# Who makes the low part of the last tile's x3: two halves on VectorE in place of GpSimd

## What is computed

```
x = x + L0(x)   # gate/up/silu/down, each with rank-16 adapters picked per batch
x = x + L1(x)   # W = weights[condition]; einsum('bct,bcd->bdt', x, W): 32 x 32 per batch
x = x + L2(x)   # x @ W.T plus SCALING * (top-2 of 8 experts, rank 16, softmax gates)
x = x + L3(x)   # as L1, with its own 16 matrices of 32 x 32
```

## Time and profile before

| | us |
|---|---|
| median of 3 runs | 585.18 |
| lowest and highest of them | 585.09, 585.28 |
| the profiled execution, as timed | 585.28 |
| its span in the profile | 583.0 |
| TensorE busy | 568.0 (97% of the span) |
| VectorE busy | 302.7 (52%) |
| ScalarE busy | 205.4 (35%) |
| GpSimd busy | 225.0 (39%) |

### The profile page before, as it was taken

How to read it: one execution, slowest core, us unless ns; L and a number is a source line. 1 busy time by engine, 2 the same in 40 slices (tenths; PEclk the granted TensorE clock), 3 DMA queues, 4 the chain that set the end, 5 groups by cost and what they waited for, 6 DMA issues and landing times.

```text
span 583.0 us, 8797 instructions
## 1 busy us (share of the span) xinstructions
PE 568.0 (97%) x3371; PEld 512.3 (88%) x3371; DVE 302.7 (52%) x695; ACT 205.4 (35%) x413; POOL 225.0 (39%) x229
## 2 busy tenths in 40 slices
PE   5989999999999999999999999999999999999996
PEld 4778998988889898989898989898989899999994
DVE  4896353535353534344444444444444657778775
ACT  4764242323233333333232323323232533333321
POOL 5442143556565656441313131413130212433422
PEclk9999999999999999999999999999999999999998
DMA  8992333343434343442424242424242911243322
GB/s 269 374 320 70 109 123 115 101 154 125 151 131 154 126 153 121 151 152 78 137 76 138 76 137 76 136 77 136 76 137 73 329 53 54 83 154 109 126 74 73
DMA packets 34889, 77.38 MB, mean 133 GB/s; under 512 B 5216, under 2 KB 9632, under 8 KB 34848
## 3 DMA queue, kind: packets, MB, share of 16 engines
q0 software_dynamic: 10752, 37.23, 20.4%
q1 hardware_dynamic: 23952, 39.56, 20.1%
q10 hardware_dynamic: 144, 0.03, 0.0%
HBM read 64.22 MB, written 12.58 MB: 132 GB/s over the span
## 4 chain that ended last, share of the span: by engine, by line
PE 94%; DMA 2%; DVE 2%; ACT 1%; issue 0%; POOL 0%; SPq 0%; DVEq 0%
PE gu_ps L1139 14%; PE gu_ps L1141 14%; PE gu_ps L1140 13%; PE down_ps L1139 8%; PE down_ps L1140 8%; PE down_ps L1141 8%; PE l_ps L1139 5%; PE l_ps L1140 5%; PE l_ps L1141 5%; PE gu_ps L1146 3%; PE gu_ps L1147 3%; PE act_t L1209 3%; DMA b_sel_raw<-b_gu,idx_rank 1%; PE x2t_ps L1263 1%; PE down_ps L1147 1%; PE down_ps L1146 1%
## 5 line engine op out<-in xcount | busy, mean ns | idle before, releaser
L666 POOL DMA_INDIRECT b_sel_raw<-b_gu,idx_rank x48 | 47.6, 992 | 189.5 <-PE gu_ps L1147 176.6
L1139 PE MATMUL gu_ps<-w_sb,xt 128*128 128x512 f32 x256 | 104.7, 409 | 0.7 <-DVE w_sb L932 0.7
L1139 PE MATMUL down_ps<-wd_sb,act_hl 128*128 128x288 f32 (+1 forms) x352 | 105.1, 299 | 0.0
L1140 PE MATMUL down_ps<-wd_sb,act_hl 128*128 128x288 f32 (+1 forms) x352 | 103.7, 295 | 0.0
L1141 PE MATMUL down_ps<-wd_sb,act_hl 128*128 128x288 f32 (+1 forms) x352 | 103.6, 294 | 0.0
L1141 PE MATMUL gu_ps<-w_sb,xt 128*128 128x512 f32 x256 | 100.6, 393 | 0.0
L1140 PE MATMUL gu_ps<-w_sb,xt 128*128 128x512 f32 x256 | 100.2, 391 | 0.0
L666 POOL DMA_INDIRECT a_raw<-a_all,idx_batch x64 | 76.5, 1195 | 58.0 <-DVE wd_sb L932 38.1
L784 ACT CAST act_hl<-act_t 128x256 fp32r<-128x256 f32 (+1 forms) x64 | 27.3, 452 | 134.6 <-PE act_t L1209 130.6
L775 ACT ACTIVATE act<-gu_ps 128x512 f32<-128x512 f32 (+1 forms) x47 | 26.1, 555 | 126.5 <-PE gu_ps L1147 126.5
L932 DVE TENSOR_TENSOR act_hl<-act_t,act_hl 128x256 fp32r<-128x256 f32 (+1 forms) x64 | 32.0, 520 | 71.8 <-ACT act_hl L784 71.0
(11 more groups left out here) (146 smaller groups left out, 1107.3 us busy)
## 6 DMA issues: line engine op xcount, KB each, us to landing
w_sb_raw<-wgu SPq DMA_DIRECT2D x16, 256.0 KB, 10.6
x_res<-x_rows SPq DMA_DIRECT2D x16, 256.0 KB
x_after_l<-x_res SPq DMA_DIRECT2D x16, 256.0 KB
bd<-bd_hl SPq DMA_DIRECT2D x16, 256.0 KB
x<-x_after_l SPq DMA_DIRECT2D x16, 256.0 KB, 2.7
bd_hl<-bd SPq DMA_DIRECT2D x16, 256.0 KB, 4.0
xt_raw<-x_t SPq DMA_DIRECT2D x15, 256.0 KB
out<-y SPq DMA_DIRECT2D x15, 256.0 KB, 2.0
```

Source lines behind the costliest of these rows:

```text
L666: nc.gpsimd.indirect_dma_start(out=dst, out_offset=None, in_=table, in_offset=bass.IndirectOffsetOnAxis(ap=idx, axis=0)).then_inc(s, 16)
L1139: pe.matmul(out_, stationary[0], moving[0], start=start, stop=False, skip_group_check=True)
L1140: pe.matmul(out_, stationary[0], moving[1], start=False, stop=False, skip_group_check=True)
```

## The change

GpSimd's `low_x3` no longer knows pieces, and its call for the last tile is gone. A new function of VectorE, `low_last_x3`, makes both halves for tile 15. It waits for the high half (s_x3hi) and, for the first half, for GpSimd's low part of tile 14 (s_x3lo at 15); for the second half it waits for its own first half (s_x3lo at 16), so that s_x3lo counts in order as before. It stands between add_x3(15) and add_y(14) in VectorE's queue.

```diff
             def low_x3(t):
-                for n, (a, b) in enumerate(pieces(t)):
-                    pool.wait_ge(s_x3hi, t + n + 1)
-                    pool.tensor_tensor(x3_hl[:, t % 2, 1, a:b], x3[:, t % 3, a:b],
-                                       x3_hl[:, t % 2, 0, a:b].bitcast(F32), ALU.subtract).then_inc(s_x3lo, 1)
+                pool.wait_ge(s_x3hi, t + 1)
+                pool.tensor_tensor(x3_hl[:, t % 2, 1, :], x3[:, t % 3, :],
+                                   x3_hl[:, t % 2, 0, :].bitcast(F32), ALU.subtract).then_inc(s_x3lo, 1)
...
                 if t < NT:
                     low_x1(t)
-            low_x3(NT - 1)
...
+            def low_last_x3():
+
+                t = NT - 1
+                for n, (a, b) in enumerate(pieces(t)):
+                    ve.wait_ge(s_x3hi, t + n + 1)
+                    ve.wait_ge(s_x3lo, t + n)
+                    ve.tensor_tensor(x3_hl[:, t % 2, 1, a:b], x3[:, t % 3, a:b],
+                                     x3_hl[:, t % 2, 0, a:b].bitcast(F32), ALU.subtract).then_inc(s_x3lo, 1)
+
...
             add_y(NT - 3)
             add_x3(NT - 1)
+            low_last_x3()
             add_y(NT - 2)
             add_y(NT - 1)
```

## The result

| | before | changed |
|---|---|---|
| median, us | 585.23 (585.09 to 585.33, 6 runs) | 583.12 (582.38 to 584.41, 6 runs) |
| ratio to before | | 0.9971, 95% interval 0.9961 to 0.9981 |
| the profiled execution, us | 585.28 | 584.41 |
| its span, us | 583.0 | 582.5 |

The changed kernel is faster by 1.7 us by the ratio (0.0029 x 585.2, interval 1.1 to 2.3) and by 2.1 us by the medians. The prediction said no change, 584.85 to 585.5.

The account below looks back on a forecast made before the run. TensorE carries 94% of the chain, but the end hangs on y of tile 14's store: 0.16 us less TensorE wait, 0.00 arriving, plus 0.84 us VectorE work hidden in idle time, gives 585.2 us, no change; range 584.85 to 585.5.

Parts of the forecast that it names:

- The end hangs on the moment at which y of tile 14 is stored: Program end: stores queue behind y of tile 14's store, which the change doesn't move; no change, 585.2 us, chance 0.67.
- GpSimd has nothing left behind tile 14: End of GpSimd's queue: without tile 15's halves no work remains there, so the added waits cost nothing else.
- Of this, 0.00 us arrives: TensorE's 0.16 us shorter wait, cut by VectorE to 0.12, by SyncE to 0.00 to 0.04, then lost at the DMA engines.
- the upper end of 0.33: TensorE's most possible gain, with the second half's load right behind the last matmul's start, 577.37; as only limit, 584.85 us.
- The 0.17 us between matmuls of 256 columns: TensorE, tile 15: spacing taken from 0.34 us between a half's first load and last matmul, used to place the second load at 577.54.
- The slack: VectorE's idle time between its second half's end, 577.11, and y of tile 14, 577.30: 0.19 us, so the addition costs nothing.
- The rival of a late VectorE: VectorE's halves overrun the slack and delay y of tile 14: 585.6 us, at worst 586.1 if blocked; chance 0.08.
- The rule that a VectorE instruction with two SBUF inputs and a GpSimd instruction that reads SBUF exclude each other: VectorE's halves: they can't meet GpSimd because the first waits for its last instruction; blocking would add 1.10 us.
- The fixed cost of about 2 us: Last store's landing: if counted from its own issue, the end moves with it; supports part of the gain arriving, chance 0.20.

Follow-up runs that it names:

- changed, late subtraction: Changed kernel plus one unread GpSimd subtraction of 128x512 that waits for both of VectorE's halves; 585.32 us against 584.67 of before, ratio 1.001.

## Why the prediction was wrong

The step that failed is the one that closed the sum: "The end hangs on the moment at which y of tile 14 is stored." It is true of the last store's landing, not of the program's end: with y of tile 14 held back by 0.99 us, SyncE's last branch came 0.9 us later (580.8 - 573.82 for 580.9 - 574.83 us after the low part of tile 14 began) and the program's end did not move. The prediction read the timeline to the end of the DMA block, 580.40, and took the 2.6 us behind it as fixed. Of these, 2.0 us were a wait of SyncE's queue, and the row that says so (SPq L259 <- PEq L259: 2.0) was in the trace of the kernel before. The sentence "GpSimd has nothing left behind tile 14" was the other half of the error: its queue still had its DRAIN, 6.3 us long in the view of line L259 and over only 5.2 us after its last subtraction.

Point by point:

- "Of this, 0.00 us arrives": right for the 0.16 us on TensorE that it spoke of. What TensorE gained was 0.41 us (last matmul 577.91 for 578.32), above the upper end of 0.33; the second half's load came at 577.28, and 577.54 was said. Two readings of the trace of before were at fault. The 0.17 us between matmuls of 256 columns is a mean over a first one that takes longer: in the changed kernel, where they follow without a gap, the spacing is 0.12. And the first half's weight load did not wait until the matmuls of tile 14 were through their spacing (577.03): it came at 576.80, with the start of the last of them, 0.28 us sooner than before, where the prediction gave 0.05. None of this reached the stores, as forecast.
- VectorE: halves from 576.25 to 577.11 forecast, 576.22 to 577.18 measured; y of tile 14 at 577.30 and y's last half at 578.24, both as forecast. The slack was 0.12 us instead of 0.19, and held. The rival of a late VectorE did not come.
- The rule that a VectorE instruction with two SBUF inputs and a GpSimd instruction that reads SBUF exclude each other (the Trainium skill, "SBUF — State Buffer", who interferes with whom) had nothing to bite on: the pair took 0.96 us, starting 0.11 us after GpSimd's last subtraction had ended. This run doesn't test it.
- The fixed cost of about 2 us (the Trainium skill, "DMA: Bandwidth & Descriptors", anatomy of one DMA) is given there for a DMA that GpSimd issues, while these stores are issued by SyncE's queue; the last one landed 1.9 us after its issue. It decided nothing: that store's issue did not move, so whether its landing follows its own issue or the bytes ahead of it stays open.
- The stores: in place within 0.01 us. Had the kernel ended with them, no change would have been right. The delayed y shows that this is a matter of what arrives last: it cost 0.7 us in the changed kernel, where the stores then bind, and nothing that can be measured in the kernel before.
- What was missing is a term: GpSimd's last instruction ends 1.54 us earlier, and about as much of the 2.0 us barrier wait goes with it. The run without any low part for the last tile measured just this, 1.54 us. The changed kernel itself gained 1.7 to 2.1 us; what may stand behind the rest is in the last section.

The cap on this gain is known too. In the changed kernel about 0.3 us are left between the arrival of SyncE's queue and the end of GpSimd's DRAIN; moving GpSimd's end further ahead by over 5 us, at the price of a y of tile 14 that is 0.36 us later, gave nothing.

## What to carry to other kernels

Follow the chain to the last instruction of the span, not to the last store: where the queue that waits for the output then waits again at the end of the block, look at each engine's DRAIN on that line and at its end, not at the name that the view gives as releaser. In a kernel like this one, give GpSimd's last work to another engine if GpSimd ends less than 5.2 us before the other queues reach the barrier; beyond that point nothing more is to be had. That an instruction at the end of GpSimd's queue is off the chain of data does not make it free.

## What the runs showed of the hardware that was not expected

GpSimd's DRAIN ends 5.1 to 5.2 us after its last instruction, in every kernel of this study (ends of the last instruction and of the DRAIN from the profiles, in us):

| kernel | last instruction | DRAIN | between |
|---|---|---|---|
| before | 577.65 | 582.8 | 5.2 |
| changed | 577.11 | 582.3 | 5.2 |
| before, one more subtraction | 578.67 | 583.8 | 5.2 |
| changed, late subtraction | 577.66 | 582.8 | 5.1 |
| no low part | 575.23 | 580.4 | 5.2 |
| both low parts on VectorE | 569.99 | 575.2 | 5.2 |
| changed, memset of one column | 576.89 | 582.1 | 5.2 |

What GpSimd does in this time no run shows. The DRAINs of ScalarE, TensorE and VectorE took 0.46, 0.67 and 0.46 us in the kernel before. GpSimd did some work in every kernel here; what its DRAIN does where it has none is not shown.

The start of the program varies by about 1 us between executions, and that is why the profiled execution of the changed kernel gained only 0.87 us: 1.50 us at its end and 0.37 us outside the span, less 1.00 us at its start. The up-projection's first matmuls, in the groups of 0 to 20 us, in the kernel before (busy us, mean ns):

```profile
L1139 PE MATMUL gu_ps<-wu_sb,xt 128*128 128x352 f32 x4 | 1.4, 349 | 0.0
```

and in the changed kernel, which has the same code there:

```profile
L1147 PE MATMUL gu_ps<-wu_sb,xt 128*128 128x352 f32 x4 | 2.0, 498 | 0.0
```

By 63 us it was 0.95 us behind, and stayed there. The time outside the span was about 2.3 us (median) in the kernels with VectorE's old program and 1.9 to 2.0 us in all with a changed one. Whether this is a part of the gain stays open, and the runs point both ways. For it: with the shorter time, eight measurements of nine (the changed kernel was measured twice) came out 0.2 to 0.6 us faster, by their medians against before, than the ends of their profiles say. The memset at the end of GpSimd's queue is one: 0.82 us measured, 0.26 us at the end of its profile. The two others with the old program of VectorE (one more subtraction, no low part) differ from their profiles by under 0.2 us. Against it: the kernel with two memsets on VectorE has the shorter time outside its span and did not become faster (ratio 1.0001, 0.9992 to 1.001). Each single difference is known to 0.5 to 0.7 us only. So the 1.5 us through GpSimd's end are shown, and the further 0.2 to 0.6 us of the changed kernel are not explained.
